# Experts stage of a vision tower: weight preparation and the attention's first unit laid into the encoder's steps

## The reference

```
h = _ln(jax.nn.relu(x @ ew1 + eb1) @ ew2 + eb2, eg, ebeta)
qkv = h @ aiw + aib
attn = jax.nn.softmax(jnp.einsum('bhqd,bhkd->bhqk', q, k) * SCALE, axis=-1)
o = jnp.einsum('bhqk,bhkd->bhqd', attn, v).transpose(0, 2, 1, 3).reshape(h.shape)
h = o @ aow + aob
```

## Time and profile before

| what | us |
|---|---|
| median of 3 runs | 4218.12 |
| lowest and highest | 4214.62, 4220.76 |
| the profiled execution | 4218.98 |
| its span, from the first instruction to the last | 4217.2 |
| TensorE busy in the span | 3707.1 (88%) |
| VectorE busy | 2840.8 (67%) |
| ScalarE busy | 2167.5 (51%) |
| GpSimd busy | 1273.5 (30%) |

### The profile page before, as it was taken

How to read it: one execution, slowest core, us unless ns; L and a number is a source line. 1 busy time by engine, 2 the same in 40 slices (tenths; PEclk the granted TensorE clock), 3 DMA queues, 4 the chain that set the end, 5 groups by cost and what they waited for, 6 DMA issues and landing times. The chain is left out here.

```text
span 4217.2 us, 98544 instructions
## 1 busy us (share of the span) xinstructions
PE 3707.1 (88%) x36068; PEld 2272.3 (54%) x36068; DVE 2840.8 (67%) x5019; ACT 2167.5 (51%) x4390; POOL 1273.5 (30%) x1076
## 2 busy tenths in 40 slices
PE   6769689988988988961999999999999958999997
PEld 4645346645655655640555555555555536666665
DVE  8956558858858857876666666666666664555555
ACT  4536437746755755765444444444444445555554
POOL 0027527726726735755000000000000002444443
PEclk8879789989999989985999999999999978999999
DMA  8910100010010010015211111111111131111111
GB/s 176 175 29 0 47 22 2 0 42 16 0 42 15 0 42 31 1 55 153 78 43 49 48 49 44 48 49 48 45 47 50 47 98 58 53 53 53 53 53 30
DMA packets 392891, 205.03 MB, mean 49 GB/s; under 512 B 151221, under 2 KB 386474, under 8 KB 392106
## 3 DMA queue, kind: packets, MB, share of 16 engines
q1 hardware_dynamic: 392354, 203.09, 18.7%
q10 hardware_dynamic: 392, 0.03, 0.0%
HBM read 145.55 MB, written 57.51 MB: 48 GB/s over the span
## 5 line engine op out<-in xcount | busy, mean ns | idle before, releaser
L1772 PE MATMUL banks<-l_w,l_xs 128*64 128x512 f16 x6240 | 721.5, 381 | 15.1 <-DVE l_xs L1820 14.2
L1772 PE MATMUL banks<-l_w,l_hs 128*64 128x512 f16 x6144 | 705.7, 379 | 1.7 <-DVE l_hs L1826 1.7
L1772 PEld LDWEIGHTS banks<-l_w,l_xs 128*64 128x64 f16 x6240 | 344.0, 110 | 330.8 <-issue 25.1
L1772 PEld LDWEIGHTS banks<-l_w,l_hs 128*64 128x64 f16 x6144 | 348.1, 110 | 316.9 <-DVE l_hs L1826 2.2
L185 POOL MEMSET h_ident<- 128x128 f32 x1 | 0.2, 204 | 1443.8 <-POOLq L80 1443.8
L1877 DVE SCALAR_TENSOR_TENSOR l_gates<-banks,l_unscale,l_bias 128x1024 f32<-128x1024 f32 x260 | 333.8, 1284 | 99.4 <-PE banks L1772 98.0
L976 POOL TENSOR_TENSOR ax_p<-ax_p,ax_ri 128x520 f32<-128x520 f32 (+1 forms) x256 | 320.0, 1251 | 267.6 <-DVE ax_ri L1173 267.6
L1933 ACT ACTIVATE l_gates<-l_gates 128x768 f32<-128x768 f32 x260 | 219.2, 843 | 351.1 <-DVE l_gates L1877 351.1
L2204 PE MATMUL banks<-h_mem,h_w 128*128 128x320 f16 x2496 | 357.7, 300 | 0.0
L2499 ACT ACTIVATE h_work<-banks,h_bias,h_factor 128x320 f32<-128x320 f32 x312 | 192.3, 616 | 261.0 <-PE banks L2204 257.1
L2204 PEld LDWEIGHTS banks<-h_mem,h_w 128*128 128x128 f16 x2496 | 245.1, 98 | 92.9 <-issue 0.3
(11 more groups left out here) (307 smaller groups left out, 7205.1 us busy)
## 6 DMA issues: line engine op xcount, KB each, us to landing
image<-in_x_dram SPq DMA_DIRECT2D x192, 196.0 KB
l_x<-x_scratch SPq DMA_DIRECT2D x130, 256.0 KB, 3.0
mem_scratch<-l_hs SPq DMA_DIRECT2D x520, 64.0 KB, 1.9
h_mem<-mem_scratch SPq DMA_DIRECT2D x104, 320.0 KB, 3.7
x_scratch<-x_out SPq DMA_DIRECT2D x4, 4160.0 KB, 16.4
raw_in<-in_L_ffn_attn_in_w_dram SPq DMA_DIRECT2D x4, 768.0 KB, 4.6
h_scratch<-x_out SPq DMA_DIRECT2D x1, 2080.0 KB, 6.5
z_scratch<-z SPq DMA_DIRECT2D x1, 2080.0 KB, 11.6
```

Of the source, the lines that this page charges most:

```text
L1772: mm = pe.matmul(ps[d * HALF:(d + 1) * HALF, 2 * z + n, :], lhsT, w_of[e][:, d, kk, b, n * 512:(n + 1) * 512], start=(kk == 0 and turn_ == ...
```

## The change

Every engine's steps are written out (`laid_steps`), and between them stand the parts of the preparation and of the attention's start, by a table from step number to function: a part with number k is issued behind the instructions of step k on its engine. On TensorE: the sums of the vectors behind step 0, those of the values behind 2, the turned and shared largest entry behind 3 and 4, and behind step 10, ahead of the last variance, the keys and queries of the first unit. On VectorE: gains behind 1, largest entry and the copy of `w_out` behind 2, its reduction behind 3, sizes behind 4, the low halves behind 6 and 7, the first unit's move and split behind 8 and 9, the second unit's move behind 10. On ScalarE the high half stands behind step 5. `w1` isn't copied any more. TensorE starts step 0 without waiting for the preparation, and ScalarE waits only for the vectors. SyncE issues the next expert's loads when all of `h` is there.

```diff
+def laid_steps(body, between):
+    for k in range(WSTEPS + LAG):
+        body(k, k % RING, lambda j, k=k: j <= k and k - j < WSTEPS)
+        if k in between:
+            between[k]()
...
+    def pe_begin(self, pe, e, ps, w_in):
+        pe.wait_ge(self.x_low, BASE + e * self.UNITS + 1)
+        self.pe_keys(pe, ps[:, 6, :], w_in, 0)
+        self.pe_queries(pe, ps[:, 5, :], w_in, 0)
...
-        pe.wait_ge(self.x_low, BASE + base + 1)
-        self.pe_keys(pe, ps[:, 6, :], w_in, 0)
-        self.pe_queries(pe, ps[:, 5, :], w_in, 0)
...
-        dve.wait_ge(self.out_kept, BASE + base * KD)
-        for lo, hi in ((0, 1), (2 * SEQ - 1, 2 * SEQ + 1), (4 * SEQ - 1, 4 * SEQ + 1)):
-            dve.memset(ps[:, 0:4, lo:hi], 0.0).then_inc(self.cleared, 1)
-        self.dve_move(dve, src, base, 0)
-        self.dve_split(dve, base, 0, base * GROUP)
-        self.dve_move(dve, src, base + 1, 1)
+        for lo, hi in ((0, 1), (2 * SEQ - 1, 2 * SEQ + 1), (4 * SEQ - 1, 4 * SEQ + 1)):
+            dve.memset(ps[:, 0:4, lo:hi], 0.0).then_inc(self.cleared, 1)
...
-                sp.wait_ge(w_low, BASE + e + 1)
+                sp.wait_ge(h_ready, BASE + (e + 1) * STEPS)
...
-                wide_steps(pool, body)
+                laid_steps(body, {})
...
+                def sum_vectors():
+                    pe.wait_ge(prep_step, BASE + e * PREP + 1)
+                    at = VECTORS["b2"][0]
...
+                    mm.then_inc(prep_sums, 1)
+                def sum_values():
+                    pe.wait_ge(prep_step, BASE + e * PREP + 8)
...
+                def turn_most():
+                    pe.wait_ge(measured, BASE + e + 1)
+                    pe.transpose(ps[0:1, 5, P:2 * P], most[:, :], ident[:, :]).then_inc(most_turned, 1)
+                def share_most():
+                    pe.wait_ge(sizing, BASE + e * SIZING + 1)
+                    pe.matmul(ps[:, 5, 2 * P:2 * P + 1], units[:, :], row_most[:, :], start=True,
+                              stop=True).then_inc(most_shared, 1)
+                def begin():
+                    pe.wait_ge(w_low, BASE + e + 1)
+                    att.pe_begin(pe, e, ps, w_in)
...
-                            pe.matmul(ps[:, m, 0:WIDE], w1[:, m * P:(m + 1) * P], z[:, ds(k * WIDE, WIDE)],
+                            pe.matmul(ps[:, m, 0:WIDE], raw_w1[:, m * P:(m + 1) * P], z[:, ds(k * WIDE, WIDE)],
...
+                        if k == 1:
+                            pe.wait_ge(prep_step, BASE + e * PREP + 5)
...
-                wide_steps(pe, body)
-                pe.wait_ge(w_low, BASE + e + 1)
+                laid_steps(body, {0: sum_vectors, 2: sum_values, 3: turn_most, 4: share_most, WSTEPS: begin})
...
                 dve.tensor_scalar(row_mean[:, :], row_sum[:, :], 1.0 / D, None, ALU.mult).then_inc(prep_step, 1)
+                dve.wait_ge(prep_step, BASE + b + 3)
+                dve.wait_ge(prep_sums, BASE + e * 3 + 1)
+                dve.tensor_reduce(b2_mean[:, :], ps[:, 5, 0:KD], AX.X, ALU.add).then_inc(prep_step, 1)
+                dve.wait_ge(prep_step, BASE + b + 6)
+                dve.tensor_scalar(b2c[:, :], V["b2"], b2_mean[:, 0:1], None, ALU.subtract).then_inc(prep_step, 1)
+                dve.wait_ge(prep_step, BASE + b + 7)
+                def gain_weights():
+                    dve.wait_ge(prep_sums, BASE + e * 3 + 2)
+                    dve.tensor_tensor(in_b[:, :], ps[:, 6, 0:3 * KD], V["in_b"], ALU.add).then_inc(prep_step, 1)
+                    for k in range(KD):
+                        dve.tensor_scalar(raw_in[:, k, :], raw_in[:, k, :], V["g"][:, k:k + 1], None,
+                                          ALU.mult).then_inc(gained, 1)
+                def measure():
+                    dve.wait_ge(gained, BASE + (e + 1) * KD)
+                    dve.tensor_reduce(most[:, :], raw_in[:, :, :], AX.XY, ALU.max,
+                                      apply_absolute_value=True).then_inc(measured, 1)
+                    dve.tensor_copy(w_out[:, :, :], raw_out[:, :, :]).then_inc(prep_step, 1)
+                def reduce_most():
+                    dve.wait_ge(prep_sums, BASE + e * 3 + 3)
+                    dve.tensor_tensor(out_b[:, :], ps[:, 7, 0:KD], V["out_b"], ALU.add).then_inc(prep_step, 1)
+                    dve.wait_ge(most_turned, BASE + e + 1)
+                    dve.tensor_reduce(row_most[:, :], ps[0:1, 5, P:2 * P], AX.X, ALU.max).then_inc(sizing, 1)
+                def size():
+                    at = e * SIZING
+                    dve.wait_ge(most_shared, BASE + e + 1)
+                    dve.tensor_scalar(bound[:, :], ps[:, 5, 2 * P:2 * P + 1], TINY, None, ALU.max).then_inc(sizing, 1)
+                    dve.wait_ge(sizing, BASE + at + 2)
+                    dve.tensor_scalar(power[:, :].bitcast(I32), bound[:, :].bitcast(I32), EXPONENT, None,
+                                      ALU.bitwise_and).then_inc(sizing, 1)
+                    dve.wait_ge(sizing, BASE + at + 3)
+                    dve.reciprocal(inv_power[:, :], power[:, :]).then_inc(sizing, 1)
+                    dve.tensor_scalar(factor[:, :], power[:, :], 1.0 / TOP / NORMED, None, ALU.mult).then_inc(sizing, 1)
+                    dve.wait_ge(sizing, BASE + at + 4)
+                    dve.tensor_scalar(w_scale[:, :], inv_power[:, :], TOP, None, ALU.mult).then_inc(sizing, 1)
+                def low_half(k):
+                    dve.wait_ge(w_high, BASE + e + 1)
+                    return dve.scalar_tensor_tensor(out=w_in[:, k, 1, :], in0=raw_in[:, k, :], scalar=w_scale[:, 0:1],
+                                                    in1=w_in[:, k, 0, :], op0=ALU.mult, op1=ALU.subtract)
+                def begin_first():
+                    dve.wait_ge(h_ready, BASE + e * STEPS + 1)
+                    att.dve_move(dve, h, e * att.UNITS, 0)
+                def begin_second():
+                    dve.wait_ge(h_ready, BASE + e * STEPS + 2)
+                    att.dve_move(dve, h, e * att.UNITS + 1, 1)
+                between = {1: gain_weights, 2: measure, 3: reduce_most, 4: size, 6: lambda: low_half(0),
+                           7: lambda: low_half(1).then_inc(w_low, 1), 8: begin_first,
+                           9: lambda: att.dve_split(dve, e * att.UNITS, 0, e * att.UNITS * GROUP), WSTEPS: begin_second}
...
-                wide_steps(dve, body)
-                dve.wait_ge(w_high, BASE + e + 1)
-                for k in range(KD):
-                    op = dve.scalar_tensor_tensor(out=w_in[:, k, 1, :], in0=raw_in[:, k, :], scalar=w_scale[:, 0:1],
-                                                  in1=w_in[:, k, 0, :], op0=ALU.mult, op1=ALU.subtract)
-                op.then_inc(w_low, 1)
+                laid_steps(body, between)
...
-                act.wait_ge(prepared, BASE + e + 1)
+                act.wait_ge(prep_step, BASE + e * PREP + 1)
...
-                wide_steps(act, body)
-                act.wait_ge(sizing, BASE + (e + 1) * SIZING)
-                act.activation(w_in[:, :, 0, :], raw_in[:, :, :], ACT.Identity, scale=w_scale[:, 0:1]).then_inc(w_high, 1)
+                def raise_weights():
+                    act.wait_ge(sizing, BASE + (e + 1) * SIZING)
+                    act.activation(w_in[:, :, 0, :], raw_in[:, :, :], ACT.Identity,
+                                   scale=w_scale[:, 0:1]).then_inc(w_high, 1)
+                laid_steps(body, {5: raise_weights})
```

70 lines of the change are left out of this document (16 added, 54 removed).

## The result

| | before | changed |
|---|---|---|
| median | 4219.44 us | 4192.11 us (4188.63 to 4193.47) |
| ratio to before | | 0.9933, 95% interval 0.992 to 0.9945 |
| profiled execution | 4218.98 us | 4191.02 us (span 4189.3) |
| granted clock, whole span | 0.939 | 0.944 |

The forecast was 4221.5 us, "same", and its range ended at 4203. The kernel became 27 us faster, 0.7%. The prediction was wrong in sign and in range.

What follows compares the result with a forecast made beforehand. Each expert's encoder steps were taken as bound by a ring through VectorE and ScalarE. Head -33, steps +37 and their end -0.4 gave +3.4 us on the profiled 4218.98: forecast 4221.5 us, "same", range 4203 to 4233.

Steps and rivals of the forecast that it cites:

- The head: Start of an expert to its first inversion: 9.3 us earlier as TensorE starts step 0 without the vectors; 33 us for four.
- Rival D: Head of an expert: branch and code fetch leave TensorE nothing to do before 865.5; +1.9 x 4, 4229 us; chance 0.09.
- Step 4: `size`... I take 2.5: VectorE's five tiny size operations behind step 4's inversion: 0.7 us alone, 2.6 held by GpSimd; 2.5 taken from a 128x3 row.
- 8 x 5.41: Encoder steps, first to ninth inversion: eight turns of the VectorE-ScalarE ring at 5.41 us each, 43.3 us before added work.
- The split 3.0: VectorE's split behind step 9: second part waits for GpSimd's multiplication; 1.1 us alone, about 3.0 held, 3.0 taken.
- the copy's step 2.5: VectorE behind step 2: largest entry 1.7 us, then the `w_out` copy waits until 2.1 and takes 0.4; 2.5 us.
- Low halves 0.83, move 0.55: VectorE behind steps 6, 7 and 8: 0.85 us for each low half, 0.6 for the first move, each first in the port.
- The ring in sum: First to ninth inversion: 44.66 us becomes 53.9 with 10.6 of added work, 9.2 us longer per expert, 37 in all.
- The end, "5.0 + 5.7 + 4.9 + 2.0": Ninth inversion to last, to class-token matmuls, to first class matmul, plus cold first unit: 17.6 us, 0.3 longer; -0.4 in all.
- A: Steps and keys: the port doesn't hold short VectorE operations and the keys run warm; 5.8 x 4, 4198.5 us; chance 0.12.
- B: End of the steps: the clock costs more, with keys, variance and first unit cold; 3.1 x 4, 4234 us; chance 0.17.
- C: End of the steps: the clock costs nothing, TensorE warm through keys, variance and first unit; 4206.5 us; chance 0.15.

Runs made afterwards that it cites:

- size3: The changed kernel with step 4's five small size operands three columns wide instead of one: 4201.6 us, 0.9959 of the kernel before.
- unroll_only: The kernel before with only its encoder steps written out, preparation and attention start left in place: 4216.2 us, 0.9987 of the kernel before.
- apart_fill1: split_apart plus two TensorE matmuls per expert that nobody reads, ahead of the second unit's keys: 4178.3 us, 0.9902 of the kernel before.
- split_apart: The changed kernel with the first unit's move behind step 5 and the split's halves behind steps 8 and 9: 4192.1 us, 0.9936 of the kernel before.
- fill_all: split_apart plus unread TensorE matmuls per expert: 15 in pauses, five ahead of the second unit's keys, five at the expert's end: 4170.2 us, 0.9887 of before.
- prep_only: The changed kernel with the first unit's moves, split, keys and queries put back behind the steps: 4193.2 us, 0.9930 of the kernel before.

## Why the prediction was wrong

Point by point, by its own steps:

- **The head: right in its path, 4.9 us short in its size.** -9.3 us predicted for the second expert, -10.2 measured; -33 in all, -37.9 measured. The path, the branch and the order of the terms hold. The 12.2 us from the first h2 to the inversion were 11.25: the clock rose earlier. Rival D is out: TensorE starts 4.05 us behind its last out matmul.
- **"Step 4: `size`... I take 2.5": wrong, 1.85 us an expert, 7.4 in all.** The step that failed is the choice of the nearest row. Width three is held, width one is not (size3).
- **"8 x 5.41": 0.7 us an expert too much.** 5.41 us is a turn of the loop. Written out, unroll_only's eight turns take 42.92 us (5.24 in five, 5.57 in three) instead of 43.3, and the change's ring is 0.4 shorter than these and what was laid between them (8.0) add up to.
- **The split 3.0, the copy's step 2.5:** 2.63 and 2.32; the mechanism was right. Low halves 0.83, move 0.55: right. The ring in sum +5.9, not +9.2.
- **The end, "5.0 + 5.7 + 4.9 + 2.0": some 3 us an expert too long (11.8 in all: -12.2 measured, -0.4 predicted), the second large miss.** Each cost of the clock was taken near its upper end. TensorE's pause was 2.31 us, not 3; the keys 4.35, not 4.8; the variance 1.56, not 2.1; so R8 to R9 was 3.2 to 3.9, not 5.0. The first score's cold start was 0.9, and the rest of the attention 0.35 in experts 2 to 4, not 2.0 together. The terms without the clock, 5.54 and 4.67, were right.
- **The rivals.** A's 4198.5 lies nearest to the 4192.1, but by chance: it was right about `size` and wrong about split and copy, which are held, and about warm keys. B is out: the matmuls are slow only up to about 940. C was nearest for the time behind mx: the change pays next to nothing there.
- **The Trainium skill's rule** (TensorE: Matmul & The Clock Gate, Part 1), that the ramp is under 1% of a typical kernel and not worth fitting to, gave C. For the change's size it was a better guide than my clock terms. Its 1% holds here too, but what lies below it can be had: apart_fill1 takes 14 us, 0.3%, off split_apart with two matmuls, and fill_all is 22 us, 0.5%, under split_apart with the same useful work.

So the terms were off by 1.2 (head), 1.85 (size), 1.1 (turn and split) and about 3 us (end) per expert, all on the same side, and four times over 28 to 30 us: the distance from +3.4 to the measured -26.5. The forecast's sign rested on -33 against +37, each of which was known no better than that.

The range failed for the same reason. It reached to the clock at no cost (4206.5), that is to one error at a time. None of the four alone would have led out of it; all four came on one side.

## What to carry to other kernels

Work between two dependent stages costs its whole length, and laid into a ring only what the ring doesn't cover: 8.3 to 10.4 us of head became 4.3 us of ring (prep_only against unroll_only, low halves included). Lay each VectorE operation that GpSimd can hold up first behind the event that also starts GpSimd, one in a step (split_apart: 1.71 us an expert off the ring). When an edit wins where it stands and the total doesn't move, compare TensorE's clock in the stretches behind it before you drop it: split_apart would have been thrown away at 0.9936, and with two more matmuls it stands at 0.9902.

## What I had not expected of the hardware

- A VectorE scaling from SBUF to SBUF waits for GpSimd with 3 elements a row (1.70 us) and not with 1 (0.13 us).
- The loop's end costs TensorE 2.9 us of pause (849.26 less the end of the last out matmul). Matmuls queued ahead of it run in this time, and 0.60 us of pause is left; they hardly bring the next work forward (0.3 us), but the clock stays up for it (fill_all).
- A TensorE pause can cost more elsewhere than where it is. Two matmuls (1.66 us) in a pause of 1.4 us were followed by 1.3 us less in the matmuls behind them, and the run fell by 14 us, of which at most 5.6 lie in the attentions where they stand. The heads 240 us later were 2.7 to 4.2 us shorter; part of that may be the spread between executions, for the first head, ahead of all added matmuls, was 2.6 shorter as well.
